# First maxima beside the projections, weight quantised in the last attention steps, five-deep output stage, in a fused attention and MXFP4 linear layer

## What is computed

```python
q, k, v = x @ Wq.T, x @ Wk.T, x @ Wv.T           # B=4, S=1024, 32 heads of 16
q, k = rope(q), rope(k)
scores = q @ k.T / 4 + bias[h, i - j]            # bias inside a band of 256, causal mask
m = maximum(max(scores), offset[h])
p = exp(scores - m)
o = (p @ v) / (sum(p) + exp(offset - m))
x = layernorm(x + o @ Wo.T)
# every 32 values share a power-of-two scale, and each value is rounded to e2m1
x = layernorm(x + mxfp4(x) @ mxfp4(weight).T + bias_ff)
```

## Time and profile before

| | us |
|---|---|
| median of 3 runs | 1794.21 (1793.2 to 1794.51) |
| the profiled execution, its own time | 1794.08 |
| its span, first to last instruction | 1792.3 |
| PE busy / DVE busy / ACT busy / POOL busy | 1639.8 / 1291.7 / 1109.9 / 249.4 |
| mean granted TensorE clock, 1 is 2.4 GHz | 0.957 |

### The profile page before, as it was taken

How to read it: one execution, slowest core, us unless ns; L and a number is a source line. 1 busy time by engine, 2 the same in 40 slices (tenths; PEclk the granted TensorE clock), 3 DMA queues, 4 the chain that set the end, 5 groups by cost and what they waited for, 6 DMA issues and landing times. The chain is left out here.

```text
span 1792.3 us, 28802 instructions
## 1 busy us (share of the span) xinstructions
PE 1639.8 (91%) x9136; PEld 762.4 (43%) x9136; DVE 1291.7 (72%) x3801; ACT 1109.9 (62%) x1596; POOL 249.4 (14%) x123
## 2 busy tenths in 40 slices
PE   7999999669999999999999999999999998777763
PEld 3444444213444444444444444444444443333321
DVE  2444544398887888888888788878888833589996
ACT  2333333205878778778887887877878886344432
POOL 4323323210000000000000000000000000244443
PEclk9999999858999999999999999999999999899995
DMA  5444444842453444335335334433533202122211
GB/s 210 141 156 155 140 160 151 193 95 48 84 85 60 84 72 73 80 64 84 80 58 90 81 53 78 93 58 66 105 57 57 53 15 76 35 77 76 70 47 47
DMA packets 124628, 157.09 MB, mean 88 GB/s; under 512 B 14928, under 2 KB 80528, under 8 KB 124240
## 3 DMA queue, kind: packets, MB, share of 16 engines
q1 hardware_dynamic: 124496, 155.45, 37.2%
HBM read 104.15 MB, written 50.46 MB: 86 GB/s over the span
## 5 line engine op out<-in xcount | busy, mean ns | idle before, releaser
L876 ACT ACTIVATE probs<-ps 128x1024 f32<-128x1024 f32 (+3 forms) x768 | 592.2, 810 | 176.7 <-PE ps L685 118.3
L1166 DVE CUSTOM_DVE_ANT_0 junk<-ps,bias_q 128x384 bf16<-128x384 f32 (+2 forms) x1024 | 501.6, 502 | 138.1 <-PE ps L660 127.6
L660 PE MATMUL ps<-k_stack,q_stack 96*128 96x384 bf16 (+3 forms) x1536 | 501.4, 344 | 30.8 <-DVE mx L1166 16.3
L679 PE MATMUL ps<-q_stack,k_stack 99*128 99x512 bf16 (+3 forms) x1536 | 489.6, 328 | 13.2 <-ACT ps L891 4.7
L1159 DVE TENSOR_REDUCE mx<-ps 128x1 f32<-128x128 f32 (+3 forms) x768 | 364.6, 485 | 42.4 <-PE ps L660 35.1
L685 PE MATMUL ps<-bias_r,ident_r 128*128 128x384 f32 (+2 forms) x1280 | 352.6, 363 | 0.0
L636 PE MATMUL ps<-attn 128*128 128x512 f32 x768 | 332.2, 595 | 10.9 <-DMA attn<-hT 9.9
L700 PE MATMUL ps<-probs,v_sb 128*32 128x512 f32 (+3 forms) x3072 | 327.3, 498 | 0.1
L660 PEld LDWEIGHTS ps<-k_stack,q_stack 96*128 96x128 bf16 x1536 | 143.0, 97 | 379.8 <-DVE mx L1166 149.8
L685 PEld LDWEIGHTS ps<-bias_r,ident_r 128*128 128x128 f32 x1280 | 222.4, 193 | 37.1 <-issue 0.3
L636 PEld LDWEIGHTS ps<-attn 128*128 128x128 f32 x768 | 146.5, 191 | 195.8 <-issue 195.8
(11 more groups left out here) (90 smaller groups left out, 1068.6 us busy)
## 6 DMA issues: line engine op xcount, KB each, us to landing
q_stack<-q_parts SPq DMA_DIRECT2D x192, 128.0 KB, 4.3
v_dram<-v_sb SPq DMA_DIRECT2D x32, 512.0 KB, 2.7
v_sb<-v_dram SPq DMA_DIRECT2D x32, 512.0 KB, 9.6
q_parts<-q_stack SPq DMA_DIRECT2D x96, 128.0 KB, 1.9
k_parts<-k_stack SPq DMA_DIRECT2D x96, 128.0 KB, 2.0
k_stack<-k_parts SPq DMA_DIRECT2D x32, 384.0 KB, 7.3
attn<-hT SPq DMA_DIRECT2D x8, 1024.0 KB, 6.3
k_stack<-k_parts SPq DMA_DIRECT2D x32, 256.0 KB, 8.0
```

The source lines that it names most:

```text
L660: pe.matmul(ps_ring[:, use.bank, 0:c1 - c0], q_stack[0:STACK, b, hl, I * P:(I + 1) * P], k_stack[0:STACK, b, hl, c0:c1], start=True, stop= ...
L679: mm = pe.matmul(ps_s[:, u % 2, hh, 0:w], k_stack[0:ROWS, b, hl, J * P:(J + 1) * P], q_stack[0:ROWS, b, hl, i0:i0 + w], start=not in_bank, ...
L876: act.activation(probs[:, (u // 2) % 3, 2 * pr:2 * pr + 2, 0:w], ps_s[:, pr, :, 0:w], ACT.Exp).then_inc(exp_done, 1)
L1166: ins = dve.tensor_tensor_reduce(out=junk[:, use.bank, 0:c1 - lo], in0=ps_ring[:, use.bank, lo - c0:c1 - c0], in1=bias_q[:, hl, BAND - t0 ...
```

## The change

**Projections and first maxima.** The maxima of the first two steps are made inside the projections of batches 2 and 3 (counted from 0): one maximum tile after the second of a projection tile's four matmuls, one after the fourth. The ring keeps banks 0 to 2, so the projections cycle over 5 banks instead of 8. DVE and POOL take up their pairs in a new order. In batch 3, V and the parts use only half of their buffers (V slot 1, part buffers 1 and 3), because the other half is already being loaded for stage 2; SP's loads are spread over batches 1 to 3. The loops of stages 1 and 3 are written out.

**Weight.** It and the feed-forward bias are loaded at the start of step 30. DVE quantises the first half of the weight after unit 4 and the second half after unit 13 of step 30, and PE transposes it in step 31 at units 6, 8, 10 and 12, through the ring; DVE copies it out.

**Output stage.** Lead 5. PE transposes `attn` itself, without ACT's copy. The linear layer's bias is split into three bf16 parts and added by PE, one more matmul per 128 tokens, so POOL's addition is gone. PE's iteration is half of the projection, the linear layer of block i, the other half, the transposes of block i+5, the quantised transposes of block i+1. `x2` has 4 buffers. DVE's first rounding step stands behind the statistics.

```diff
+PBANKS = 5
+FIRST_ORDER = [(0, k) for k in range(NM)] + [(1, k) for k in range(4)] + [(0, "M")] + [(1, k) for k in range(4, NM)]
+        return pair % 4 if pair < PAIRS - 8 else 1 + 2 * (pair % 2)
+        return pair % 2 if pair < PAIRS - 8 else 1
-LEAD = 4
+LEAD = 5
...
+            def loads_beside(b, q):
+                if (b, q) == (1, 2):
+                    sp.wait_ge(ones_set, 1)
+                    wait_parts(8)
+                    load_stack(0, 0, 0)
+                    sp.wait_ge(ext_stored, 16 * 2)
+                    for hl in range(HG):
+                        load_bias_q(0, hl)
+                    load_bias_k(0)
+                if (b, q) == (2, 2):
+                    wait_parts(16)
+                    load_stack(0, 1, 1)
+                if (b, q) == (3, 2):
+                    wait_parts(24)
+                    load_stack(0, 2, 2)
+                if (b, q) == (3, 4):
+                    sp.wait_ge(v_stored[0], FIRST + 16 * v_uses(24)[0])
+                    sp.wait_ge(v_stored[1], FIRST + 16 * v_uses(8)[1])
+                    load_v(0, 0, 0)
+                if (b, q) == (3, 1):
+                    load_shift(0, 0)
...
+            def beside_projection(b, i, half):
+                if b < 2:
+                    return
+                n = b - 2
+                if (n, i, half) == (1, 2, 0):
+                    transpose_shift(0, Use.first(0, "M"))
+                maxima(0, n, [2 * i + half], lambda k: Use.first(n, k))
+            def project(b, c, i):
+                tile = b * 24 + c * 12 + i
+                if tile >= PBANKS:
+                    old = tile - PBANKS
+                    pe.wait_ge(v_ready if old % 3 == 2 else raw_ready, FIRST + old // 3 + 1)
...
+                    mm = pe.matmul(ps[:, RING + tile % PBANKS, :], lhsT, rhs, start=(kt == 0), stop=(kt == NK - 1))
+                    if kt == 1:
+                        beside_projection(b, c * 12 + i, 0)
+                mm.then_inc(proj_done, 1)
+                beside_projection(b, c * 12 + i, 1)
...
             def iteration(at):
-                for work, t in ((transpose_attn, at(4)), (out_projection, at(4)),
-                                (transpose_quantised, at(1)), (linear, at(1))):
+                if at(4).exists:
+                    out_projection(at(4).s, at(4).par, 0)
+                if at(0).exists:
+                    linear(at(0).s, at(0).par)
+                if at(4).exists:
+                    out_projection(at(4).s, at(4).par, 1)
+                if at(5).exists:
+                    transpose_attn(at(5).s, at(5).par)
+                if at(1).exists:
+                    transpose_quantised(at(1).s, at(1).par)
...
             def iteration(at):
-                if at(4).exists:
-                    copy_attn_T(at(4).s, at(4).par)
-                if at(5).exists:
-                    copy_attn(at(5).s, at(5).par)
                 t = at(3)
                 if t.exists:
                     root(0, t.s, t.par, ln1_steps, std1)
                     normalise1(t.s, t.par)
+                if at(5).exists:
+                    copy_attn_T(at(5).s, at(5).par)
                 if at(1).exists:
                     copy_quantised_T(at(1).s, at(1).par)
                 t = at(0)
...
-                pool.tensor_tensor(x2b[par], x2[par], bff_sb.unsqueeze(1).broadcast_to([P, W3, DM]),
-                                   ALU.add).then_inc(x2b_ready, 1)
...
+            def turn_pair(b, pair):
...
+                for i in range(3):
+                    maximum(i)
+                dve.wait_ge(raw_ready, FIRST + done + 1)
+                dve.tensor_tensor(by_cos, raw[:, q % 2, :, :],
...
+                maximum(3)
...
+                if pair:
+                    third_part(done - 1)
+                maximum(4)
...
+                dve.tensor_tensor(rest, rot[:, q % 2, :, :], part_bufs[buf][:, 0, :, :],
+                                  ALU.subtract).then_inc(rest_ready, 1)
+                maximum(5)
...
                 if ln.exists:
                     residual1(ln)
-                rounding(0)
-                if ln.exists:
                     dve.wait_ge(y_read, FIRST + ln.s + 1)
                     row_stats(0, yv[ln.par], ln1_steps)
+                rounding(0)
                 rounding(1)
```

More of the change, by code:

```diff
@@ L125, in ring_order @@
                 order += [(b, k) for ks in units_beside(u) for k in ks]
-            if not (first and b == 0) and u == MT_LEFT and not (last and b > B - AHEAD):
+            if u == MT_LEFT and not (last and b > B - AHEAD):
                 order.append((b - 1, "M"))
@@ L131, in ring_order @@
                 order.append((b, "O0"))
+            if last and b == B - 1 and u in W_UNITS:
+                order.append((b, f"W{W_UNITS.index(u)}"))
         if last and b == B - 1:
@@ L745, in phase2 @@
                         maxima(ga, ba, behind, use_of)
-                        if left and u == MT_LEFT and not (last and b > B - AHEAD):
+                        if u == MT_LEFT and not (last and b > B - AHEAD):
                             transpose_shift(n + 1, use_before("M"))
@@ L825, in _, with projections @@
             start_counters(act, [raw_ready, v_ready, exp_done, o_copied, at_evac, a_evac, out_ready])
[L827 removed]
+            def projections(b):
                 def take_up(pair):
[L830 to L832 removed]
+                    q = pair % 4
+                    tile = b * 24 + 3 * pair
+                    bank = RING + tile % PBANKS
+                    act.wait_ge(proj_done, tile + 2)
                     act.wait_ge(raw_read_dve, FIRST + b * 8 + pair - 1)
@@ new lines, in _ @@
+            for b in range(B):
+                if b == 2:
+                    dve.wait_ge(off_loaded, 16)
+                    dve.tensor_scalar(neg_off[:, :], off[:, :], -1.0, None, ALU.mult).then_inc(neg_off_ready, 1)
+                    dve.wait_ge(neg_off_ready, 1)
+                    dve.wait_ge(ident_ready, 4)
+                for pair in range(8):
+                    turn_pair(b, pair)
+                third_part(8 * b + 7)
+                if b >= 2:
+                    shifts(0, b - 2, b - 2, Use.first(b - 2, NM - 1))
@@ new lines, in take_weight_T, with phase2, use_of, use_before @@
+            def take_weight_T(kt, use):
+                dve.wait_ge(ring_filled, use.before + 1)
+                dve.tensor_copy(wq_T[:, kt, :], ps_ring[:, use.bank, :].bitcast(BF16)[:, 0:DM])\
+                    .then_inc(ring_read, 1)
+            def phase2(g, kind):
+                last = kind == LAST_GROUP
+                for b in range(B):
+                    n = g * B + b
+                    ga, ba = ahead(g, b)
+                    more = not (last and b >= B - AHEAD)
+                    left = b or kind != FIRST_GROUP
+                    def use_of(what):
+                        return Use(g, b, what, kind)
+                    def use_before(what):
+                        return Use(g, b - 1, what, kind)
+                    for u in range(NU):
+                        inner, behind = units_beside(u) if more else ((), ())
+                        for ks in (inner, behind):
+                            for k in ks:
+                                max_unit(ga, k, ba % 2, use_of(k))
+                        if u == MT_LEFT and not (last and b > B - AHEAD):
+                            dve.wait_ge(shift_loaded[b], 16 * PARTS * (g + 1))
+                            split_shifts(n + 1, use_before("M"))
+                        if more and u == SPREAD - 1:
+                            shifts(ga, n + 2, ba % 2, use_of(NM - 1))
+                        if left and u == OT_LEFT:
+                            normalise(*before_in(g, b), n - 1, 1, use_before("O1"))
+                        if last and b == B - AHEAD and u == OT_LEFT:
+                            weight_half(0)
+                        if u == OT_0:
+                            normalise(g, b, n, 0, use_of("O0"))
+                            if last and b == B - AHEAD:
+                                weight_half(1)
+                                bias_parts()
+                        if last and b == B - 1 and u in W_UNITS:
+                            take_weight_T(W_UNITS.index(u), use_of(f"W{W_UNITS.index(u)}"))
+                    if last and b == B - 1:
+                        normalise(g, b, n, 1, use_of("O1"))
```

479 lines of the change are left out of this document (218 added, 261 removed).

## The result

The changed kernel takes **1764.95 us** (median of 4, 1762.07 to 1767.04); the kernel before, on the same chips, 1794.36. The ratio is 0.984 (95% interval 0.982 to 0.985): 29 us faster, half of the 60 I forecast, and above the range of 1722 to 1747.

A forecast was written before the change was run, and what follows sets the result against it. Projections were taken as bound by PE, stage 2 by PE and ACT, stage 3 by DVE. Gains 37 + 1 - 1 + 17 + 0 + 6 = 60 us took 1794 to 1734, range 1722 to 1747 (chance 0.57).

The forecast's parts named there:

- the twelve full iterations: Stage 3: loop through ACT's root at 14.0 us, 14.6 with clock loss; 173.3 against 173.1, 0 gained, bounds +28 and -15.
- the term for the clock: Stage 3 full iterations: 0.6 us added on average, for 1.2 to 1.7 us lost in some four of ten.
- The rival with low clock in every iteration: Stage 3: clock low for 3.2 us each iteration, 16.0 us apart; 15 us more, 1749; chance 0.15.
- X = 27.6 us: Projections of stage 1: end 27.6 us later, at 370.2, from 16.6 + 5 + 3 + 3.
- 96 tiles and the ring: Projections: maximum tiles cost PE 0.17 us each, 16.6 in all; waits for DVE's bank add 5 over 16 pairs.
- The store of V behind stack 2: Projections, batch 3: a stack's nine loads delay the store about 7 us, ACT waits some 5, PE loses 3.
- three signs that I had named for being wrong: Residuals in stage 3 standing 12 us apart, residuals standing 16 apart, or batch 3 taking more than 100 us.
- Filling: Start of stage 3: fourth residual at +38.9 us instead of 55.9 after the step's end; 17 us gained, bounds 14 and 20.
- emptying: End of stage 3: three iterations lose about 2.1 us each, bias matmuls cost 0.9; 6 us gained, bounds 4 and 8.
- the maxima behind the projections: Stage 1 rival: stack 0 late, maxima run after projections, 38 us stay, 1772; chance 0.12 together with the V stall.
- the low clock in whole pairs: Batches 2 and 3 rival: PE at 1.2 GHz throughout, 165 us of projections double, 1899, slower than before; chance 0.03.
- The stall on V: Batch 3 rival: two loads cost 13.8 us each, pairs another microsecond; 35 us, about 1769; chance 0.12 together with late maxima.

## Why the prediction was half right

Of the 33 us that are missing, 19 lie in the twelve full iterations and 11 in the projections.

**The full iterations: the step that failed.** The loop was right: base 14.4 where I worked out 14.0, its wait 1.85 where I had some 2, its pause 3.39 where I had 3.35. What failed is the term for the clock. I added 0.6 us an iteration, for 1.2 to 1.7 us in some four of ten. The slow stretch came in eight of twelve and cost 1.7 us in two of them and 2.7 in six, 1.6 on average over all twelve. That is 13 of the 19 us by which the twelve iterations missed. The other 6 are the base, 0.4 us longer than I had in each, and the last iteration, which I had put at 12.7 without transposes of `attn` and which took 14.25. The rival with low clock in every iteration, at a chance of 0.15, had the right period of 16.0, in part by luck: it had every iteration 2.0 us over a base of 14.0, and the runs show only eight slow ones, most of them 2.7 us over a base of 14.4. I had both halves of the argument in hand, rows 10 with 1.13 us of work ahead of a fall, and a new pause with no work at all on the path, and leaned on the sparse stretches that leave the clock up, though the new pause is emptier than they are, as I wrote myself. The Trainium skill's section (TensorE: Matmul & The Clock Gate, A second HAM failure mode), which I had set aside for want of a run, describes such a swing between the two levels through short idle spells, in another kernel. The traces here agree: behind a pause of 3.39 us the clock fell in eight of eleven cases, behind one of 1.40 in none.

**The projections: the right mechanisms, one mis-sized and one not seen.** Of X = 27.6 us:
- 96 tiles and the ring, 21.6 us, measured 16 x 1.39 = 22.2 (11.69 less 10.30 a pair). Right. The whole 0.17 us of a tile is paid, though not by columns alone.
- The border of batches 2 and 3, 3 us, measured 1.5.
- The store of V behind stack 2, 3 us, measured 8.0. I had priced the nine loads as a delay of the store's issue alone, and let it land in the usual 2.7 us. It was issued 14.3 us behind `raw`, where I had 17, but took 9.6 us to land behind the loads. The next copy of V came 8.4 us late where I had 5 (the 11.05 of the profile hold some 2.6 in which PE's tile wasn't ready either), and PE paid nearly all of it. The 1.7 us that half a clock adds in the next four records (3.62 less 1.88) is part of it.
- The start of batch 2, not in the sum, 6.5 us. I wrote that the loads of batch 1 stay covered by two V buffers. They don't: ACT waited 8.3 us there, DVE was late, and the late DVE met the new ring. In the kernel before, ACT waited 16.21 us for such a store in batch 3 and PE's pairs stayed 10.30 us apart, and in the run with the maxima behind the projections, with five banks, waits of ACT of up to 6.42 us left them there too. Now a projection stands behind a maximum that waits for DVE.

Together 38.2. Two of the three signs that I had named for being wrong came: residuals 16 us apart on average, and a batch 3 of 103 us.

**The rest.** From the last projection to the seed, 9.0 us measured, 8.8 forecast. Stage 2 is 1.3 us longer where I forecast 1, but by luck. The weight cost 0.2 us: from the first exponential of step 30 to the end of the stage it is 61.3 us before and 61.6 after. The first exponential came 1.05 us behind the seed instead of 2.32, as forecast, and then the first step lost 2.0 us, with a granted clock of 0.70 in its first 10 us where the kernel before had 0.88. Filling 15.4 (17) and emptying 5.5 are within 2 us; my own terms for emptying, 3 x 2.1 less 0.9, give 5.4 and not 6. No maxima fell behind the projections, and the granted clock was 1.00 from 197 to 341 us, so neither the maxima behind the projections nor the low clock in whole pairs came. The stall on V came, but at 8.0 us milder than its rival had it. In both places that failed the clock came on top of waits that I had priced, or found, as time alone: after 3.39 us in most iterations, after 4.83 and 5.88 us in the projections.

## What to carry to other kernels

When an edit lets an engine pass its old bound, write out the new loop of one iteration with every in-order engine, and look for the pause it gives TensorE: a pause without any work in it can be paid twice, as time and as clock. On an engine that works in order, put the small operation that another engine waits for ahead of the long copies that nobody waits for yet; here six lines were worth some 40 us. When DVE and POOL work side by side, pair POOL's long operations with DVE reductions, statistics or PSUM reads, and keep tensor-scalar operations and those with two SBUF inputs, even of two elements, out from under them.

## What the runs showed of the hardware that I had not expected

- A two-element DVE operation takes 2.33 us when it starts 0.03 us after a POOL tensor operation, 0.16 otherwise.
- Ten matmuls that nobody reads make this kernel 18 us faster in one place of PE's iteration, and 30 us slower two steps earlier.
- A pause of PE of 3.39 us was followed by 1.2 GHz in eight of eleven cases, and in eleven of eleven when 2.3 us of work was added elsewhere; one of 1.95 us in five of seven (the last rounding step on POOL); one of 1.40 us in none. Why three of eleven kept the clock stays open.
- A store of V that lands in 2.7 us by itself took 9.6 us behind nine loads on the same queue, and 13.3 behind fourteen.
- A bf16 matmul between fp32 ones costs 0.11 us with 16 columns and 0.22 with 512.
- 1.1 us of difference in a DMA wait became 5 us at the end of the projections, through one pause that took the clock down and one that did not.
